# Self attention 1 computed with keys on partitions and four heads in array tiles, and the values of cross attention 1 projected half a chunk later

## The reference, cut to what matters

```python
# cross attention 1: 16 heads of 32 (x is also rounded to an int8 grid before wq, the output before wp)
q = qdq(x) @ qdq(wq).T + bq
k, v = jnp.split(cond @ wkv.T + bkv, 2, axis=-1)          # cond: 4096 x 512
attn = softmax(einsum('bnhd,bmhd->bhnm', q, k) * scale)   # 16 x 256 x 4096
out = qdq(einsum('bhnm,bmhd->bnhd', attn, v)) @ qdq(wp).T + bp

# self attention 1: 32 query heads of 16, 8 key/value heads, each shared by 4 query heads
q = (x @ wq) ; k = repeat(x @ wk, 4) ; v = repeat(x @ wv, 4)
scores = einsum('bhqd,bhkd->bhqk', q, k) / sqrt(16)       # 32 x 256 x 256
amask = where((j >= i - 256) & (j < i), -1e10, 0)         # query i sees only keys j >= i
out = einsum('bhqk,bhkd->bqhd', softmax(scores + amask), v) @ wo
```

## Time and profile before

| | us |
|---|---|
| median of 3 runs | 1645.35 |
| the profiled execution | 1643.54 |
| its span, first to last instruction | 1641.4 |
| first pass of cross attention 1 | 861.0 to 1107.0 |
| self attention 1, from its first projection to its last addition | 1300.8 to 1406.7 |

### The profile page before, as it was taken

One profiled execution on the slowest core, in us unless ns is written; L12 is line 12 of the kernel. 1 busy time (PEld: TensorE's weight loads), 2 busy tenths in 40 slices (PEclk: granted clock), 3 DMA queues, 4 the chain that ended last, 5 costly groups with the idle time before them and its releaser, 6 DMA issues. The chain is left out here.

```text
span 1641.4 us, 33418 instructions
## 1 busy us (share of the span) xinstructions
PE 1500.4 (91%) x12154; PEld 1138.3 (69%) x12158; DVE 1118.6 (68%) x1946; ACT 821.9 (50%) x1302; POOL 190.8 (12%) x128
## 2 busy tenths in 40 slices
PE   5999999999979899999849999958999699889998
PEld 3677776777745389999738777735665455689997
DVE  5766666666632478888674777766998376466664
ACT  2677777777741454444222222217887166355452
POOL 0000000000010323333221111110000034000000
PEclk8999999999989989999969999978999799899999
DMA  3111111111020065454124333218774200376662
GB/s 135 40 42 36 44 38 40 39 38 38 13 104 6 12 237 176 168 183 158 39 107 135 112 112 115 103 52 178 171 174 103 84 1 1 111 260 212 216 218 74
DMA packets 59560, 169.27 MB, mean 103 GB/s; under 512 B 6370, under 2 KB 22546, under 8 KB 55891
## 3 DMA queue, kind: packets, MB, share of 16 engines
q1 hardware_dynamic: 59492, 168.36, 32.8%
HBM read 149.41 MB, written 17.33 MB: 102 GB/s over the span
## 5 line engine op out<-in xcount | busy, mean ns | idle before, releaser
L457 ACT ACTIVATE x_probs<-psum 128x1024 f32<-128x1024 f32 x256 | 248.2, 1022 | 12.9 <-PE psum L340 3.7
L175 PE MATMUL psum<-m_x_hi,m_gu_hi 128*128 128x256 f32 (+1 forms) x816 | 233.3, 286 | 5.4 <-DVE m_h L2141 2.8
L176 PE MATMUL psum<-m_x_hi,m_gu_lo 128*128 128x256 f32 (+1 forms) x816 | 232.2, 285 | 0.0
L177 PE MATMUL psum<-m_x_lo,m_gu_hi 128*128 128x256 f32 (+1 forms) x816 | 231.9, 284 | 0.0
L175 PE MATMUL psum<-x_w_hi,x_ctx_hi 128*128 128x256 f32 (+1 forms) x640 | 211.8, 331 | 10.8 <-DVE x_ctx_lo L484 10.8
L176 PE MATMUL psum<-x_w_hi,x_ctx_lo 128*128 128x256 f32 (+1 forms) x640 | 194.9, 305 | 0.0
L177 PE MATMUL psum<-x_w_lo,x_ctx_hi 128*128 128x256 f32 (+1 forms) x640 | 194.6, 304 | 0.0
L1337 DVE TENSOR_REDUCE x_peaks<-psum 128x2048 f32 (+1 forms) x64 | 146.7, 2291 | 56.7 <-PE psum L1273 56.7
L175 PEld LDWEIGHTS psum<-x_w_hi,x_ctx_hi 128*128 128x128 f32 x640 | 121.4, 190 | 74.4 <-issue 59.0
L175 PEld LDWEIGHTS psum<-m_x_hi,m_gu_hi 128*128 128x128 f32 (+1 forms) x816 | 153.2, 188 | 8.1 <-DVE m_h L2141 3.2
L176 PEld LDWEIGHTS psum<-m_x_hi,m_gu_lo 128*128 128x128 f32 (+1 forms) x816 | 153.2, 188 | 1.2
(11 more groups left out here) (294 smaller groups left out, 2851.8 us busy)
## 6 DMA issues: line engine op xcount, KB each, us to landing
m_gu_raw<-in_m_gu SPq DMA_DIRECT2D x18, 1408.0 KB, 6.0
m_gu_raw<-in_m_gu SPq DMA_DIRECT2D x32, 768.0 KB, 4.3
x_k_stack<-x_keys_dram SPq DMA_DIRECT2D x45, 512.0 KB, 6.9
x_ctx_raw<-in_ctxT SPq DMA_DIRECT2D x64, 256.0 KB, 2.6
m_dn_raw<-in_m_down SPq DMA_DIRECT2D x16, 768.0 KB, 4.3
m_dn_raw<-in_m_down SPq DMA_DIRECT2D x18, 512.0 KB, 3.8
x_ctx_raw<-in_ctxT SPq DMA_DIRECT2D x16, 512.0 KB, 4.0
x_keys_dram<-x_keys_hi SPq DMA_DIRECT2D x16, 512.0 KB, 3.2
```

The source lines that it names most:

```text
L175: pe.matmul(out, a[0], b[0], start=start, stop=False, skip_group_check=True)
L176: pe.matmul(out, a[1], b[0], start=False, stop=False, skip_group_check=True)
L177: return pe.matmul(out, a[0], b[1], start=False, stop=stop, skip_group_check=True)
L457: act.activation(probs[:, grp, :], g.psum[:, 2 + 2 * (grp % 2):4 + 2 * (grp % 2), :].rearrange("p b n -> p (b n)"), ACT.Exp).then_inc(prob ...
```

## The change

Self attention 1 no longer calls `attention_core`. Keys are projected once for the 8 key heads (4 matmuls instead of 16) and go through DRAM into a `k_pad` in which four copies stand at partitions 0, 32, 64 and 96; `q_pad` holds the queries so that the four query heads of one key head stand in these four row groups. `tops` computes scores with queries on partitions, with the mask added by a bf16 matmul, only to get each row's maximum; the negative maxima are turned and written by four DMAs into a 17th row of each group of `q_pad`, whose partner in `k_pad` is 1. `score` then computes scores minus maximum with keys on partitions, only over the half that the mask lets through (384 of 512 columns), ScalarE makes the exponentials of four heads in one instruction, and `weigh` multiplies them with the values and with ones (the sums) in four column tiles. One reciprocal and one multiplication per pair of key heads follow, and the projection runs chunk by chunk. `wo` is loaded after the rearranging DMAs and no longer with the other weights. On the host, columns of `wq` and rows of `wo` are reordered.

```diff
+        J, PAIRS, SEEN = B_H // B_KV, B_KV // 2, L + P
...
+        ORDER = list(range(0, B_KV, 2)) + list(range(1, B_KV, 2))
+        acc = g.bank[4:8]
...
+            @block.sync
+            def _(sp):
+                sp.wait_ge(k_cleared, 1)
+                sp.wait_ge(k_taken, 1)
+                sp.dma_start(keys_dram, kT[:, :]).then_inc(k_stored, 16)
+                sp.wait_ge(k_stored, 16)
+                for j in range(J):
+                    sp.dma_start(k_pad[32 * j:32 * j + B_HD, :, :],
+                                 keys_dram.rearrange("(n d) k -> d n k", d=B_HD)).then_inc(k_placed, 16)
+                sp.wait_ge(q_taken, 2)
+                for j in range(J):
+                    sp.dma_start(q_pad[32 * j:32 * j + B_HD, 1::2, :],
+                                 q_pad[32 * j + B_HD:32 * j + 2 * B_HD, 0::2, :]).then_inc(q_placed, 16)
+                sp.dma_start(wo[:, :, :], A["a1_wo"]).then_inc(wo_loaded, 16)
+                sp.wait_ge(q_placed, 16 * J)
+                sp.wait_ge(peak_taken, 1)
+                for j in range(J):
+                    sp.dma_start(q_pad[32 * j + B_HD:32 * j + B_HD + 1, :, :],
+                                 peakT[B_KV * j:B_KV * j + B_KV, :]).then_inc(peak_placed, 16)
...
+                pool.memset(k_pad[:, :, :], 1.0).then_inc(k_cleared, 1)
+                pool.memset(mask[:, :, :], 0.0).then_inc(mask_cleared, 1)
+                pool.tensor_copy(ident16[:, :], g.ident[:, :])
...
+                pool.wait_ge(mask_cut, 2)
+                pool.tensor_copy(mask16[:, :, 0, :], mask[:, :, :])
+                pool.tensor_copy(mask16[:, :, 1, :], mask[:, :, :]).then_inc(mask_made, 1)
...
+                def tops(i):
+                    n = ORDER[i]
+                    if i >= 2:
+                        pe.wait_ge(tops_read, i - 1)
+                    banks = g.bank[4 * (i % 2):4 * (i % 2) + 4]
+                    for t in range(NT):
+                        for j in range(J):
+                            pe.matmul(banks[j][:, t * L:t * L + L - t * P],
+                                      q_pad[32 * j:32 * j + B_HD, n, t * P:(t + 1) * P],
+                                      k_pad[32 * j:32 * j + B_HD, n, t * P:L], start=(t == 0), stop=False,
+                                      skip_group_check=True)
+                    for j in range(J):
+                        last = pe.matmul(banks[j].rearrange("p (t k) -> p t k", t=NT)[:, :, 0:P], ident16[:, :],
+                                         mask16[:, 0, :, :], start=False, stop=True, skip_group_check=True)
+                    last.then_inc(tops_ready, 1)
+                def score(n):
+                    if n:
+                        pe.wait_ge(probs_ready, n)
+                    for kt, at in ((1, 0), (0, L)):
+                        for j in range(J):
+                            rows = slice(32 * j, 32 * j + B_HD + 1)
+                            wide = P * (kt + 1)
+                            pe.matmul(g.bank[j][:, at:at + wide], k_pad[rows, n, kt * P:(kt + 1) * P],
+                                      q_pad[rows, n, 0:wide], start=(kt == 1), stop=False, skip_group_check=True)
+                    for j in range(J):
+                        last = pe.matmul(g.bank[j][:, P:SEEN], ident16[:, :],
+                                         mask16[:, 1, :, :].rearrange("p a k -> p (a k)"), start=False, stop=True,
+                                         skip_group_check=True)
+                    last.then_inc(scores_ready, 1)
+                def weigh(n):
+                    pe.wait_ge(probs_ready, n + 1)
+                    p, a = n // 2, n % 2
+                    for at_out, w in ((0, None), (L, ones_pad[:, a, :])):
+                        for kt, at in ((1, 0), (0, L)):
+                            wide = P * (kt + 1)
+                            for j in range(J):
+                                last = pe.matmul(acc[p][32 * j:32 * j + 32, at_out:at_out + wide],
+                                                 v_pad[:, kt, n, :] if w is None else w,
+                                                 probs[:, n % 2, j, at:at + wide], start=False, stop=False,
+                                                 skip_group_check=True)
+                    last.then_inc(pv_done, 1)
+                def project(c):
+                    pe.wait_ge(divided, c + 1)
+                    for t in range(NT):
+                        last = pe.matmul(g.bank[t][:, :], outT[:, c, t * P:(t + 1) * P], wo[:, c, :],
+                                         start=(c == 0), stop=(c == NC - 1))
+                        if c == NC - 1:
+                            last.then_inc(out_done, 1)
...
+                pe.wait_ge(mask_made, 1)
+                pe.wait_ge(k_placed, 16 * J)
+                pe.wait_ge(q_taken, 2)
+                for i in range(B_KV):
+                    if i == B_KV // 2:
+                        pe.wait_ge(q_placed, 16 * J)
+                    tops(i)
                 pe.wait_ge(wv_loaded, 16)
+                pe.wait_ge(tops_read, B_KV - 1)
...
+                pe.wait_ge(tops_read, B_KV)
+                for t in range(NT):
+                    last = pe.transpose(g.bank[2][0:B_H, t * P:(t + 1) * P], peak[:, t, :], g.ident[:, :])
+                last.then_inc(peak_turned, 1)
+                for b in acc:
+                    pe.matmul(b, g.zeros[:, 0:P], g.zeros[:, :], start=True, stop=False, skip_group_check=True)
+                pe.wait_ge(v_cleared, 2)
+                pe.wait_ge(v_taken, 1)
+                pe.wait_ge(peak_placed, 16 * J)
+                score(0)
+                for n in range(B_KV):
+                    if n + 1 < B_KV:
+                        score(n + 1)
+                    weigh(n)
+                pe.wait_ge(wo_loaded, 16)
+                for c in range(PAIRS):
+                    project(c)
+                dve.tensor_copy(kT[:, :], g.bank[0][:, 0:L]).then_inc(k_taken, 1)
+                for i in range(B_KV):
+                    n, at = ORDER[i], 4 * (i % 2)
+                    dve.wait_ge(tops_ready, i + 1)
+                    for t in range(NT):
+                        last = dve.tensor_reduce(
+                            peak[:, t, :].rearrange("p (j n) -> p j n", n=B_KV)[:, :, n:n + 1]
+                            .rearrange("p j n -> p (j n)"),
+                            g.psum[:, at:at + 4, t * L:t * L + L - t * P], AX, ALU.max)
+                    last.then_inc(tops_read, 1)
+                dve.wait_ge(peak_turned, 1)
+                dve.tensor_scalar(peakT[:, :], g.bank[2][0:B_H, 0:L], -1.0, None, ALU.mult).then_inc(peak_taken, 1)
+                for p in range(PAIRS):
+                    dve.wait_ge(pv_done, 2 * p + 2)
+                    dve.reciprocal(inverse[:, p % 2, :], acc[p][:, L:2 * L]).then_inc(inverted, 1)
+                    dve.wait_ge(inverted, p + 1)
+                    dve.tensor_tensor(outT[:, p, :], acc[p][:, 0:L], inverse[:, p % 2, :],
+                                      ALU.mult).then_inc(divided, 1)
+                for t in range(NT):
+                    dve.wait_ge(out_done, t + 1)
+                    dve.tensor_tensor(g.x[:, t, :], g.x[:, t, :], g.bank[t][:, :], ALU.add)
+                    act.wait_ge(q_done, b + 1)
+                    act.activation(q_pad[:, 4 * b:4 * b + 4:2, :], g.bank[6 + b].rearrange("p (m q) -> p m q", m=2),
+                                   ACT.Copy, scale=B_HD ** -0.5).then_inc(q_taken, 1)
...
+                for n in range(B_KV):
+                    act.wait_ge(scores_ready, n + 1)
+                    if n >= 2:
+                        act.wait_ge(pv_done, n - 1)
+                    act.activation(probs[:, n % 2, :, :], g.psum[:, 0:4, 0:SEEN], ACT.Exp).then_inc(probs_ready, 1)
```

```diff
+                    def keys_of(k, s, w):
+                        j = key_unit(k, s, w)
+                        o = g.bank[4 + (2 * s + w) % 4]
+                        if w == 0:
+                            pe.wait_ge(ctx_split, 2 * k + s + 1)
+                        pe.wait_ge(unit_taken, j + 1)
+                        for m in (2 * w, 2 * w + 1):
+                            for c in range(NC):
                                 last = product3(pe, o[:, (m % 2) * L:(m % 2 + 1) * L],
                                                 [b[:, c, m * P:(m + 1) * P] for b in (w_hi, w_lo)],
                                                 [b[:, s, c, :] for b in (ctx_hi, ctx_lo)], c == 0, c == NC - 1)
+                        last.then_inc(unit_done, 1)
+                    def values_of(k, s, t):
+                        o = g.bank[4 + (2 * s + t) % 4]
+                        pe.wait_ge(unit_taken, value_unit(k, s, t) + 1)
+                        for c in range(NC):
+                            last = product3(pe, o[:, :], [b[:, s, c, t * P:(t + 1) * P] for b in (ctx_hi, ctx_lo)],
```

(35 more changed lines are left out.)

233 lines of the change are left out of this document (93 added, 140 removed).

## The result

The changed kernel takes 1597.87 us, the median of 4 runs (1594.90 to 1598.86), against 1645.34 of the kernel before on the same chip (4 runs, 1642.90 to 1645.55): a ratio of 0.9712, 95% interval 0.9695 to 0.9729. The forecast was 1601 us, its range 1594 to 1608. The profiled execution took 1598.19 us, its span 1596.4, 45.0 less than before's.

A forecast was written before the change was run, and what follows sets the result against it. Mostly TensorE was taken to bound the kernel. Self attention 1 would save 34.1 us and pass 1 10.2, together 44.3 off the profiled 1643.54 (1599.2); with the median 1.8 higher, 1601 us, range 1594 to 1608.

The forecast's parts named there:

- What bounds it: Self attention 1's core: TensorE's float32 matmuls and transposes; pass 1: TensorE in the loop, a score-reduction handshake in the last chunk.
- Front: Self attention 1's start: projections, with keys' way through DRAM ending level with the queries; `tops` starts 12.1 us in.
- Tops: Row maxima in self attention 1: VectorE's reductions bind at 1.8 us per key head, 16.0 us in all.
- Turning point: Between `tops` and loop: uncovered chain of transposes, scaling, four small DMAs and handing over, 6.0 us.
- Loop: Self attention 1: score and exponential alternate, 3.2 us a head, plus last `weigh` and 2.5 us half-clock start; 29.8 us.
- Rival (c): Shorter loop with free switches and short hand-overs: 2.7 us a turn, turning point 5, total 1596 us; chance 0.11.
- End: Self attention 1's output projection and last addition, 7.9 us; last reciprocal and multiplication lie under matmuls.
- Pass 1: First pass of cross attention 1: 11.0 us less ahead of the loop, minus 0.3 and 0.5; 10.2 us less.
- rival (e): First pass of cross attention 1: the 11 us return as late splits, 1.5 us a body, total 1611 us; chance 0.07.
- (a): In `tops` and `score`, float32 row groups don't run side by side: 28 us given back, total 1629 us; chance 0.08.
- (b): Half clock in `tops` (+8 us) and far into the loop (+5 us), total 1614 us; chance 0.12.
- (d): Pass 1 bodies wait for late context loads, making the kernel slower than before; 1657 us at 21 us landing; chance 0.02.

The follow-up runs named there:

- one_bank_set: The changed kernel, but in the last body of the first pass all scores go to banks 0 to 3, without the second set; median 1599.8 us.
- fill_in_tops: Changed kernel with one DMA for the maxima, 7 zero matmuls in that wait, context split on ScalarE and GpSimd, plus two zero matmuls per head in `tops`; 1590.39 us.
- split_off_vector: The changed kernel, but in the first pass's loop ScalarE rounds the context and GpSimd makes its low part, so VectorE only reduces; 1594.14 us.
- one_row_group: The changed kernel, but in `tops` and `score` all four matmuls read row group 0, with number, shape and order kept; 1665.89 us.
- no_mask_in_score: The changed kernel, but `score` leaves out its four mask matmuls and ScalarE copies instead of taking exponentials; 1596.95 us (two runs).
- with_fill_in_norms: Changed kernel with one maxima DMA, 7 zero matmuls there, context split on ScalarE and GpSimd, plus 10 zero matmuls in every layer norm; 1592.60 us.

## Why the prediction was right, point by point

*What bounds it.* Right in both stages. The views gave the time because each touched stretch had one engine that never stopped, or one handshake. That the total came so near was luck in part: the profiled execution gained 45.0 us where 44.3 were forecast, but from 1.0 more in self attention 1, 1.5 less in pass 1, 3.4 in a stage where nothing was forecast, and 2.2 lost elsewhere.

*Front.* 12.1 us forecast, 12.7 measured; keys, their way through DRAM and the queries do end together (the last wait is for ScalarE's `q_pad`, 0.78 us; in one_bank_set it is the keys' DMAs).

*Tops.* 16.0 forecast, 15.5 measured, VectorE's reductions 13.95 for 14.4. *Turning point.* 6.0 against 5.4; four issues of 0.70 us and the landing.

*Loop.* 29.8 against 29.3, but by two errors that cancel. A turn is 3.02 us and not 3.2 (8 x 0.18 = 1.4 us too much): 1.51 from scores to exponential where I had 1.6, and 1.51 for the exponential with its hand-over where I had 1.6, since that hand-over takes 0.05 us and not 0.15. The last `weigh` took 1.4 for 1.7. The charge for changes of mode, 0.17 us each, was not far off: some 0.1 for leaving the whole array and, by the estimate under fill_in_tops, 0.19 for leaving row tiles. The Trainium skill's rule that a change of mode drains the engine ("TensorEngine Tiling (Array Packing)", Key Properties) agrees with that; it gives no price. The 4 us that I had for free changes were too many by my own sum: `weigh`'s change lies under the exponential, and the two a head that lie on the path are 2.7 us. Rival (c) had changes free, which they are not, and its turn of 2.7 us did not come. The start at half clock was sized at 2.5 us and took (4.17 - 3.02) + (4.44 - 3.02) = 2.6 between exponentials, and 1.1 before the first (2.67 us from first matmul to exponential instead of 1.5 to 1.6): 3.7, 1.2 more.

*End.* 7.9 and 7.9. The reciprocal took 1.76 us where I estimated 1.9:

```profile
1357.34 1.76 DVE L1096 RECIPROCAL a_inverse<-psum 128x256 f32<-128x256 f32 x1 [2.41 <-PE psum L1020]
1359.13 0.42 DVE L1098 TENSOR_TENSOR a_outT<-psum,a_inverse 128x256 f32<-128x256 f32 x1
1363.52 0.69 DVE L1102 TENSOR_TENSOR x_res<-x_res,psum 128x512 f32<-128x512 f32 x1 [3.96 <-PE psum L1029]
```

VectorE is done with both at 1359.55 and then waits 3.96 us for the projection: hidden, as forecast.

*Pass 1.* The term that was mis-sized is that bodies 0 to 6 stay as they were, with +0.3 for one split: measured 7 x 0.26 = 1.8 us. VectorE in the kernel after, a body's second to eighth reduction:

```profile
913.55 2.29 DVE L1473 TENSOR_REDUCE x_peaks<-psum 128x2048 f32 x1 [1.10 <-PE psum L1389]
915.76 0.68 DVE L1459 CAST x_ctx_hi<-x_ctx_raw 128x1024 fp32r<-128x1024 f32 x1
916.47 1.23 DVE L1461 TENSOR_TENSOR x_ctx_lo<-x_ctx_raw,x_ctx_hi 128x1024 fp32r<-128x1024 f32 x1
917.61 2.29 DVE L1473 TENSOR_REDUCE x_peaks<-psum 128x2048 f32 x1
920.63 2.29 DVE L1473 TENSOR_REDUCE x_peaks<-psum 128x2048 f32 x1 [0.73 <-PE psum L1389]
...
924.70 2.28 DVE L1473 TENSOR_REDUCE x_peaks<-psum 128x2048 f32 x1
927.69 2.29 DVE L1473 TENSOR_REDUCE x_peaks<-psum 128x2048 f32 x1 [0.72 <-PE psum L1389]
931.20 2.29 DVE L1473 TENSOR_REDUCE x_peaks<-psum 128x2048 f32 x1 [1.21 <-PE psum L1389]
934.69 2.29 DVE L1473 TENSOR_REDUCE x_peaks<-psum 128x2048 f32 x1 [1.20 <-PE psum L1389]
```

Two items with a split in them take 7.08 us over value units (913.55 to 920.63) and 7.06 over key units (920.63 to 927.69), while without a split two items take 6.78 with values and 7.00 with keys (the pitch of 3.49 from 931.20 to 934.69 is one such item). Two items with a split take some 7.07 us whatever the units, so a split costs 0.30 beside values and 0.06 beside keys. In the kernel before, each half of the body made keys, then values, and both splits stood beside keys. Now the first stands beside values. The trace of before could have told me. Its seventh body has only one split, and two items over key units take 6.99 us there with it (reductions from 1054.82 to 1061.81) and 6.99 without (1068.58 to 1075.57); with a split in an earlier body they take 7.08. The failed words of the step are "late as before": it was not 0.3 us before. That is rival (e)'s mechanism at a sixth of its price (0.26 us a body for 1.5). split_off_vector confirms it: without splits the body is 27.54, the 27.56 of the units alone.

Ahead of the loop: 27.8 us from the first split to the first reduction before (861.16 to 889.00), 19.7 after (862.49 to 882.20). Of these 8.1 us less, 2.8 more belong to the value unit that now stands in the body ahead of that reduction: 10.9 for the 11.0 forecast. With that unit the last body is 22.0 + 2.8 = 24.8 us long where it was 24.4: +0.4 for +0.5. Sum: -10.9 + 1.8 + 0.4 = -8.7.

*m1.* Nothing was forecast, and 3.4 us came. Stretches of the same work of the kernel after, then of the kernel before (from 0.0, 9.9, 34.9 and 40.9 us after self attention 1's end; the one left out has clock 1.00 in both):

```profile
1365.10:1375.00 9.90, 5.07 (x23) 4.70 (x23) 5.28 (x10) 3.03 (x3) 0.69 (x1) 0.69 0.65 246
1375.00:1387.00 12.00, 11.78 (x84) 11.25 (x85) 9.14 (x27) 6.45 (x12) 0.00 (x0) 0.83 0.39 132
...
1400.00:1406.00 6.00, 3.73 (x27) 3.21 (x26) 4.86 (x6) 5.31 (x7) 0.00 (x0) 1.00 0.66 241
1406.00:1410.00 4.00, 4.00 (x35) 4.00 (x35) 3.06 (x4) 1.24 (x2) 0.00 (x0) 1.00 0.93 281
```

```profile
1406.70:1416.60 9.90, 5.00 (x23) 4.63 (x23) 5.22 (x11) 3.03 (x3) 0.72 (x1) 0.58 0.65 245
1416.60:1428.60 12.00, 11.78 (x79) 11.25 (x80) 8.96 (x26) 5.87 (x11) 0.00 (x0) 0.78 0.38 132
...
1441.60:1447.60 6.00, 3.21 (x15) 2.50 (x14) 3.52 (x4) 4.97 (x7) 0.00 (x0) 0.85 0.54 212
1447.60:1451.60 4.00, 4.00 (x29) 4.00 (x29) 3.94 (x5) 0.78 (x1) 0.00 (x0) 0.79 0.88 333
```

The clock rises earlier (0.69 and 0.83 for 0.58 and 0.78), and a second fall, 0.85 and 0.79 in the last two stretches, is missing. The two profiles with the old self attention have `m1` at 233.8 and 233.6 us, one_row_group at 232.3, no_mask_in_score at 231.7 and the ten others with the new one at 229.6 to 230.4. So the gain belongs to what stands before `m1`; which feature of it moves the clock there is open. The mere moment at which `m1` starts doesn't seem to decide: the ten start it up to 15 us apart and agree within 0.8 us. No step of mine had it; without it the median would have been 1597.87 + 3.4 = 1601.3.

*Rivals.* (a) is refuted: 0.87 us for sixteen instructions. Its price was set too low as well: I had 28 us for float32 row groups that don't overlap, and one_row_group gives 68, since the clock falls with it. (b) did not come in the two profiles of the kernel as it is, but did in one_bank_set and with_fill_in_norms, where `tops` took 6 us more (8 in the rival) and the stage 4 and 7 more in place of 13. In these two profiles the queries had been projected at full clock (7.07 and 7.08 us; 7.97 to 8.38 in the ten others with the new stage), and TensorE then waited 1.67 and 1.82 us for the keys (0.78 to 0.96 in the others). Of those ten only one_row_group had a fall in `tops`. That the longer wait brings the fall is likely by these rows, and not shown: no run changed it alone. (d) never showed: the bodies never waited for a load.

## What to carry to other kernels

Small matmuls that use 16 or 32 rows of the array belong in row groups four at a time, also in float32; before counting on them, ask what their columns cost one after the other, since that is what a misplaced operand brings back. Place a piece of work that makes one engine late beside the longest item of the engine that waits, not in the middle of the short ones. And after a gain in work, look at where the low clock now falls: in the profile taken with the norms filled, it had moved into a stretch that it made bound by TensorE, and the gain went there.

## What the runs showed of the hardware that was not expected

The granted clock fell to 0.56 with TensorE busy 33.52 of 34.0 us, 29.5 of them with matmuls that read one row group of 32 (one_row_group): being busy, as the trace counts it, does not by itself hold the clock. Nor does spreading over four row groups bring it back: in one_bank_set TensorE was busy all of the 17.8 us from 1310.17 to 1328.00, on `tops` in four row groups, at a granted clock of 0.50. Sixteen matmuls of zeros in 3.62 us gave the next scores the full clock and put the fall off by some 3 us only. A reciprocal of 256 elements a partition takes 1.76 us on VectorE, 6.9 ns an element, where the multiplication beside it takes 0.42. A change of mode away from the whole array costs some 0.1 us (four masks in 0.44 us without it and 0.54 with it); for one away from row tiles there is the estimate of 0.19.
